# Gated cross attention with experts on one core: x turned before it is combined, keys roped in PSUM, values kept in wide rows, and the last jobs and steps in another order

## What is computed

```python
def attention(x, ctx, mask, wq, wk, wv, wo):
    q = (x @ wq).reshape(bs, sq, 32, 128).transpose((0, 2, 1, 3))
    k = (ctx @ wk) ...   # 8 heads, each repeated for 4 query heads
    v = (ctx @ wv) ...
    q = _apply_rope(q, 0)    # x * cos + rotate_half(x) * sin
    k = _apply_rope(k, 0)
    attn = softmax(einsum('bhqd,bhkd->bhqk', q, k) / sqrt(128) + mask)
    out = einsum('bhqk,bhkd->bhqd', attn, v)
    return out.transpose(...).reshape(bs, sq, 4096) @ wo

def experts(x, route_w, A, Bw):   # 8 experts of rank 16, the best one of each token
    topk_v, topk_idx = top_k(einsum('bsd,ed->bse', x, route_w), 1)
    weight = one_hot(topk_idx) * topk_v
    return einsum('bser,eor->bso', weight * einsum('bsd,erd->bser', x, A), Bw)

x = x + tanh(g_xattn) * attention(layernorm(x), ctx_4096, ...)
x = x + tanh(g_ffn) * experts(layernorm(x), ...)
```

## Time and profile before

| | us |
|---|---|
| median of 3 runs | 1132.73 |
| lowest, highest | 1132.55, 1134.85 |
| the profiled execution | 1134.35 |
| its span in the trace | 1132.6 |
| TensorE busy | 1103.6 |
| VectorE busy | 899.3 |
| ScalarE busy | 630.8 |
| GpSimd busy | 619.2 |

### The profile page before, as it was taken

How to read it: one execution, slowest core, us unless ns; L and a number is a source line. 1 busy time by engine, 2 the same in 40 slices (tenths; PEclk the granted TensorE clock), 3 DMA queues, 4 the chain that set the end, 5 groups by cost and what they waited for, 6 DMA issues and landing times.

```text
span 1132.6 us, 17085 instructions
## 1 busy us (share of the span) xinstructions
PE 1103.6 (97%) x5664; PEld 923.1 (82%) x5664; DVE 899.3 (79%) x1407; ACT 630.8 (56%) x1096; POOL 619.2 (55%) x519
## 2 busy tenths in 40 slices
PE   7999999989999999999999999999999999999998
PEld 6788888768888888888888778888888888888875
DVE  6975748877877878788778999877887888778887
ACT  6453446566666666666666545455555555555443
POOL 4751458868777777777764433343444443443423
PEclk9999999989999999999999999999999999999999
DMA  6869955476464646464559735453535353533201
GB/s 221 264 235 361 340 163 214 140 270 231 139 230 148 233 145 225 147 215 160 174 189 375 263 127 169 152 177 102 190 122 197 121 187 114 177 110 105 75 1 75
DMA packets 93510, 206.27 MB, mean 182 GB/s; under 512 B 8816, under 2 KB 41712, under 8 KB 87536
## 3 DMA queue, kind: packets, MB, share of 16 engines
q1 hardware_dynamic: 93424, 205.18, 53.3%
HBM read 122.31 MB, written 82.84 MB: 181 GB/s over the span
## 4 chain that ended last, share of the span: by engine, by line
PE 64%; DVE 14%; POOL 10%; issue 7%; ACT 4%; DMA 0%; DVEq 0%; SPq 0%; ACTq 0%; POOLq 0%
PE attn L896 20%; PE proj L830 17%; PE score L847 7%; PE attn L782 6%; POOL rot L1680 4%; PE score L782 3%; PE turned L782 3%; POOL wq_s L1655 2%; PE attn L881 2%; PE turned L858 2%; PE attn L883 2%; DVE q_r L1140 2%; DVE q_r L1098 1%; DVE row_sum L1169 1%; DVE wo_s L1093 1%
## 5 line engine op out<-in xcount | busy, mean ns | idle before, releaser
L896 PE MATMUL attn<-wo_s,o_s 128*128 128x512 f32 x1524 | 374.6, 395 | 0.8 <-DVE o_s L1189 0.8
L830 PE MATMUL proj<-xB,wq_s 128*128 128x512 f32 x1344 | 337.1, 394 | 4.2 <-ACT copies L1466 2.2
L896 PEld LDWEIGHTS attn<-wo_s,o_s 128*128 128x128 f32 x1524 | 280.9, 188 | 57.9 <-DVE o_s L1189 1.4
L830 PEld LDWEIGHTS proj<-xB,wq_s 128*128 128x128 f32 x1344 | 252.9, 189 | 58.5 <-ACT copies L1466 2.6
L1680 POOL TENSOR_TENSOR rot<-rot,tab 128x512 f32<-128x512 f32 x112 | 170.3, 1521 | 174.2 <-ACT rot L1445 174.0
L847 PEld LDWEIGHTS score<-k_r,q_r 128*128 128x128 f32 x1024 | 124.1, 193 | 13.6 <-DVE q_r L1103 8.0
L1444 ACT ACTIVATE rot<-q_r 64x512 f32<-64x512 f32 x86 | 54.2, 630 | 143.0 <-DVE q_r L1140 138.2
L847 PE MATMUL score<-k_r,q_r 128*128 128x64 f32 x1024 | 123.5, 274 | 3.2 <-DVE q_r L1103 3.2
L1181 DVE TENSOR_TENSOR p_low<-turned,p_high 64x512 fp32r<-64x512 f32 x128 | 88.0, 688 | 40.4 <-ACT p_high L1482 38.4
L1490 ACT ACTIVATE o_s<-attn 128x512 fp32r<-128x512 f32 x127 | 69.3, 595 | 77.6 <-PE attn L883 77.6
L1103 DVE TENSOR_TENSOR q_r<-q_r,rot 128x512 f32<-128x512 f32 x86 | 89.0, 1035 | 17.0 <-POOL rot L1680 11.8
(11 more groups left out here) (230 smaller groups left out, 1702.7 us busy)
## 6 DMA issues: line engine op xcount, KB each, us to landing
wq_kept<-wq_s SPq DMA_DIRECT2D x16, 1792.0 KB, 6.3
wq_s<-wq_kept SPq DMA_DIRECT2D x16, 1792.0 KB, 8.4
v_kept<-vst SPq DMA_DIRECT2D x64, 256.0 KB, 4.7
v_s<-v_kept SPq DMA_DIRECT2D x128, 128.0 KB, 4.9
wo_kept<-wo_s SPq DMA_DIRECT2D x32, 512.0 KB, 3.7
wo_s<-wo_kept SPq DMA_DIRECT2D x32, 512.0 KB, 5.3
k_kept<-kst SPq DMA_DIRECT2D x32, 256.0 KB, 2.0
wq_raw<-in_wq SPq DMA_DIRECT2D x16, 512.0 KB, 5.5
```

The source lines that it names most:

```text
L830: last = e.matmul(dst[:, :], wq_s[:, b % 2, A, s, kt, :], xB[:, B, mv, kt, :], start=(first and kt == 0 and m == 0), stop=(kt == 1 and m = ...
L896: last = e.matmul(out_bank(k, bp)[:, :], o_s[:, s, bp, h, :], wo_s[n % WO_SLOTS][:, m, :], start=(h == 0 and i == 0), stop=(h == GROUP - 1 ...
```

## The change

- **x.** `turn_x` turns raw normalised x: 4 transposes of c0 into proj0, 4 of c1 into proj1. ScalarE copies both back to the pair's buffer (`x_copies`), GpSimd combines the turned tiles, and ScalarE and VectorE split c0, the combinations and half of c1 from SBUF (`x_split`). The steps of a pair stand 3 (turn, copy), 4 (combine) and 5 jobs (split) behind its norm, before 1 (combine) and 4 (turn, split). Pairs stand beside other jobs, two more places for x lie in far_raw[0], and xB's stores move.
- **Keys.** The cosine is made in place in the PSUM bank; the sum reads the bank and writes kst. The bank is free with the sum (`rope_added`), no longer with the cosine. Keys and values of chunk 1 alternate in `JOBS`.
- **Values.** `v_kept` holds rows of four heads: a store writes 2 KB rows; a load takes one head out of them, in pieces of 512 B.
- **Order in the jobs.** VectorE: q sums first, then behind job 56 the sum of the key before, then the bank of this job; the row sums of the first softmax ahead of job 63's bank. GpSimd: subtraction, half of a weight combination and division within job 62, the zeroing behind them in job 63. Four slots until job 63. ScalarE copies the middle product of step 0 ahead of its shifts.
- **The expert's weight** is a scalar_tensor_tensor with `best` spread over 8 columns as second tensor.
- **Last steps.** In step 60, GpSimd takes the last q's sine ahead of the second subtraction, VectorE the cosine ahead of `add_out`. At the end GpSimd waits for all norms (`ln_done`) before it adds the expert outputs of tiles 10 and 11 (`add_mixes`, which issues L1771).

```diff
...
-JOBS = [*keys_of(0), *values_of(0), *keys_of(1), *values_of(1), *values_of(2), *values_of(3), *keys_of(3), *keys_of(2)]
...
+BOTH_1 = [job for pair in zip(keys_of(1), values_of(1)) for job in pair]
+JOBS = [*keys_of(0), *values_of(0), *BOTH_1, *values_of(2), *values_of(3), *keys_of(3), *keys_of(2)]
...
-X_BESIDE = {8: 4, 11: 5, 13: 6, 16: 7, 32: 0, 35: 1, 38: 2, 41: 3}
-X_COMBINE, X_TURN, X_PLACES = 1, 4, 3
...
+X_TURN, X_COMBINE, X_SPLIT = 3, 4, 5
...
+             58: [(2, 0), (2, 1)], 60: [(2, 2)], 61: [(2, 3)]}
...
-FOUR_UNTIL, ZEROS_BESIDE = 60, 62
+FOUR_UNTIL, ZEROS_BESIDE = 63, 63
...
-    v_kept = nc.dram_tensor("v_kept", (ALL_CHUNKS, KV_HEADS, 2, P, CHUNK_TILES, DH), F32, kind="Internal").ap()
+    v_kept = nc.dram_tensor("v_kept", (ALL_CHUNKS, 2, 2, P, CHUNK_TILES, 4 * DH), F32, kind="Internal").ap()
...
-            for i, b in enumerate(proj):
-                yield b[:, :].rearrange("p (b k t) -> p b k t", b=2, k=2), [
-                    xB[:, 2 * i:2 * i + 2, part, :, cols] for part in range(2)]
...
+            for first, n, src in ((B11, 2, c0[:, :].rearrange("p (b k t) -> p b k t", b=2, k=2)),
+                                  (T1, 2, combined[:, 0:2]), (T3, 2, combined[:, 2:4]),
+                                  (B22, 1, c1[:, 2 * P:].rearrange("p (b k t) -> p b k t", b=1, k=2))):
+                yield src, [xB[:, first:first + n, part, :, cols] for part in range(2)]
...
-                                    vst[:, n % VST, part, :].rearrange("p (g d) -> p g d", g=4).bitcast(F32)).then_inc(
-                                        v_stored[n % VST], 16)
+                        e.dma_start(v_kept[i, ch, part, :, tt, :], vst[:, n % VST, part, :].bitcast(F32)).then_inc(
+                            v_stored[n % VST], 16)
...
+                                    v_kept[index, g // 4, part, TWIN_ROWS[twin], :, cols]).then_inc(v_in[u % 2], 16)
...
 
...
-                        e.wait_ge(times_cos, ROPE_NO[before] + 1)
+                        e.wait_ge(rope_added, ROPE_NO[before] + 1)
...
             def turn_x(pair):
...
                 e.wait_ge(ln_done, NORM_NO[X_PAIRS[pair][1]] + 1)
-                for i in range(4):
-                    b = (proj + [small])[i]
+                for c, w in enumerate(X_PAIRS[pair]):
                     if X_NO[pair]:
-                        e.wait_ge(x_low, 4 * X_NO[pair] - 4 + i + 1)
-                    if i == 0:
...
-                        e.wait_ge(x_combined, 4 * X_NO[pair] + 4)
-                        last = turn(b, 0, T[:, (i - 1) * 512:i * 512], cols=4)
...
-                    last.then_inc(x_turned, 1)
+                        e.wait_ge(x_copied, 2 * X_NO[pair] - 1 + c)
+                    turn(proj[c], 0, x_place(w), cols=KT).then_inc(x_turned, 1)
...
-            def rope_add(r, dst):
...
-                e.tensor_tensor(dst, dst, by_seq(rotated(r)), ALU.add).then_inc(rope_added, 1)
+                e.tensor_tensor(dst, src, by_seq(rotated(r)), ALU.add).then_inc(rope_added, 1)
...
+                    by_cos(ROPE_NO[job], by_seq(b[:, :]), by_seq(b[:, :]))
...
-            def finish_key(job):
...
                 if job[0] == "k":
-                    rope_add(ROPE_NO[job], by_seq(kst[:, K_NO[job] % KST, :]))
...
+                    rope_add(ROPE_NO[job], by_seq(kst[:, slot, :]), by_seq(kv_banks[n % 4][:, :]))
...
-                    e.tensor_scalar(weight, ranks, rank, best, ALU.is_equal, ALU.mult).then_inc(weight_set, 1)
+                    e.scalar_tensor_tensor(out=weight, in0=ranks, scalar=rank, in1=best.to_broadcast([P, EXPERTS]),
+                                           op0=ALU.is_equal, op1=ALU.mult).then_inc(weight_set, 1)
...
+                for q in SUMS_BESIDE.get(n, ()):
+                    q_sum(*q)
+                if n > KEYS_3_MADE:
+                    finish_key(n - 1)
+                if n > SCORES_AFTER:
+                    sum_rows(0)
+                finish_job(n)
                 if n == SCORES_AFTER:
                     mask_scores(0)
-                for q in SUMS_BESIDE.get(n, ()):
-                    q_sum(*q)
-                finish_job(n)
...
                 for w in SPLITS_BESIDE.get(n + 1, ()) if n + 1 < KEYS_3_MADE else ():
                     raw_low(w)
-                finish_key(JOBS[n])
-                for w in SPLITS_BESIDE.get(n, ()) if n >= KEYS_3_MADE else ():
-                    raw_low(w)
+                if n < KEYS_3_MADE:
+                    finish_key(n)
                 if n in ROPE_BESIDE:
                     q = ROPE_BESIDE[n]
                     by_cos(ROPE_NO["q", *q], q_tile(*q), q_tile(*q))
...
-                if n - X_TURN in X_BESIDE:
-                    x_lows(X_BESIDE[n - X_TURN])
-            sum_rows(0)
+                for w in SPLITS_BESIDE.get(n, ()) if n >= KEYS_3_MADE else ():
+                    raw_low(w)
+                if n - X_SPLIT in X_BESIDE:
+                    x_lows(X_BESIDE[n - X_SPLIT])
...
+                if k == 0:
+                    finish_key(len(JOBS) - 1)
...
+            q_cos(*q)
             add_out(k - 1, 0)
-            q_cos(*q)
...
+            def x_copies(pair):
+                for c, w in enumerate(X_PAIRS[pair]):
+                    e.wait_ge(x_turned, 2 * X_NO[pair] + c + 1)
+                    e.activation(x_place(w), proj[c][:, :], ACT.Copy).then_inc(x_copied, 1)
...
-                    x_highs(X_BESIDE[n - X_TURN])
+                    x_copies(X_BESIDE[n - X_TURN])
+                if n - X_SPLIT in X_BESIDE:
+                    x_highs(X_BESIDE[n - X_SPLIT])
...
+                for p in middle if k == 0 else ():
+                    copy_product(*p)
                 for q in ropes[0]:
                     q_shift(*q)
-                for p in middle:
+                for p in middle if k else ():
...
-                e.wait_ge(ln_done, NORM_NO[X_PAIRS[pair][1]] + 1)
+                e.wait_ge(x_copied, 2 * no + 2)
...
-                if n == ZEROS_BESIDE:
-                    e.wait_ge(rope_added, FOUR.stop)
-                    e.memset(p_low[:, :, :, :].bitcast(F32), 0.0).then_inc(zeros_set, 1)
-                if n == SCORES_AFTER:
-                    subtract_max(0)
...
-                if n - X_COMBINE in X_BESIDE:
-                    combine_x(X_BESIDE[n - X_COMBINE])
...
                 if JOBS[n][0] == "k":
                     by_sin(ROPE_NO[JOBS[n]])
+                if n - X_COMBINE in X_BESIDE:
+                    combine_x(X_BESIDE[n - X_COMBINE])
...
-            normalise(0)
+                if n == SCORES_AFTER:
+                    subtract_max(0)
+                    combine_weights(HEAD_PAIRS + 1, (0,))
+                    normalise(0)
+                if n == ZEROS_BESIDE:
+                    e.wait_ge(rope_added, FOUR.stop)
+                    e.memset(p_low[:, :, :, :].bitcast(F32), 0.0).then_inc(zeros_set, 1)
+            combine_weights(HEAD_PAIRS + 1, (1,))
...
                         by_sin(ROPE_NO["q", *q])
...
+            by_sin(ROPE_NO["q", Q_BLOCKS - 1, 3])
             subtract_max(k + 1)
-            by_sin(ROPE_NO["q", Q_BLOCKS - 1, 3])
             normalise(k + 1)
...
             add_mixes(k + 2)
 
...
```

82 lines of the change are left out of this document (43 added, 39 removed).

## The result

The changed kernel takes 1119.41 us (median of 4 runs, 1118.62 to 1120.93), the kernel before 1133.79 (median of 4, 1132.55 to 1138.88). Forecast was 1118.3 us, taken from the first three runs of the kernel before (median 1132.73); from there the gain is 13.3 us, and a fourth run of 1138.88 moved the median to 1133.79. The profiled execution of the changed kernel took 1119.15 us, 1117.2 of them its span.

The account below looks back on a forecast made before the run. The prediction took TensorE, busy 97% of the span, to bound the kernel. Its terms, 5.2 + 2.9 + 4.8 + 0.7 - 0.3 + 0.2 + 1.4 - 0.5 = 14.4 us, came off 1132.73 to give 1118.3 us, range 1110 to 1126.

Follow-up runs that it names:

- n_probs: The changed kernel with step 0's probabilities split first, ahead of q (1,3)'s shift on ScalarE and its sum on VectorE: 1120.86 us, ratio 0.9886 to the kernel before.
- after_again: The changed kernel run once more, with no edit, beside others on the same chip: 1120.49 us, ratio 0.9889 to the kernel before.
- u_wide: The changed kernel with the old order in step 60 (GpSimd's second subtraction ahead of the last sine, VectorE's cosine behind add_out): 1118.54 us, ratio 0.9866 to the kernel before.
- u_tail: The changed kernel without GpSimd's wait for all norms ahead of its last sums (tiles 10 and 11): 1121.73 us, ratio 0.9894 to the kernel before.
- u_order: The changed kernel with the old order in jobs 57 to 63 and step 0, keys still roped in PSUM: 1123.64 us, ratio 0.9919 to the kernel before.

## What to carry to other kernels

When an edit shortens an instruction that another engine's passes hold up and are held up by, follow both engines to every wait of the bound engine, not only the waits that name the engine edited; then ask which waits two edits would each remove, since they are gained once and can be booked to the wrong one. For the check, cut the bound engine's timeline at instructions that all kernels share and compare stretches: here the sharpest stretch repeated to 0.03 us and the long one in the middle to 0.3, where two medians of the same kernel differed by 1.1 (1119.41 and 1120.49). And when an instruction is moved out of one wait's way, look for where that wait goes: n_probs moved one of 2.74 us and gained nothing.

## What the runs showed of the hardware

TensorE's clock does not follow from the order alone. Behind the wait of 2.75 us, with the same instructions ahead of it, the granted clock fell in after_again and did not in u_wide:

```profile
225.00:229.00 4.00, 3.08 (x10) 2.61 (x11) 3.55 (x6) 2.37 (x5) 2.96 (x3) 0.68 0.95 289
```

```profile
225.00:229.00 4.00, 2.78 (x14) 2.42 (x15) 3.75 (x6) 2.26 (x5) 3.27 (x3) 1.00 0.98 305
```

The first is a mix of the levels 1.2 and 2.4 GHz, the second 2.4 throughout; the stretch to turn 5 is 62.23 and 60.65 us. The same holds at the last q: in nine executions with the same order there and a wait of 2.08 to 2.12 us, the stretch from turn 59 to turn 63 is 40.28 to 42.77 us. In u_tail (40.30) the granted clock was 1.00 behind the wait, in u_order (42.77) 0.57. My estimate from these rows: a forecast of such a wait should carry 1.5 to 2.5 us of chance.

And a pass of VectorE over two SBUF tiles and one of GpSimd don't only delay each other once: in the kernel before, six rope sums in a row take 1.77 or 1.78 us, from 20.99 to 38.9 us, and the sines beside them 1.74 or 1.75.
